# Folding a bias row and a corner product into one product, and moving half of the second norm's statistics

## The reference

```python
mod = (silu(c) @ wmod).reshape(8, 6, 1, -1)            # sa, ca, ga, sb, cb, gb
h = layernorm(x) * (1 + ca) + sa
attn = einsum('ds,td->st', w1, w2) * sparse_mask       # 1024 x 1024, non-zero near the diagonal
x = x + ga * gelu(einsum('bds,st->bdt', h, attn) + b2)
h = layernorm(x) * (1 + cb) + sb
P = h @ U1; H = P @ V1 + b1                            # 1024 -> 256 -> 2 x 2752
Z = (silu(gate) * up) @ U2; out = Z @ V2 + b2f         # 2752 -> 256 -> 1024
x = x + gb * out
```

## Time and profile before

| | |
|---|---|
| median of 3 runs | 1170.33 us (1170.17 to 1173.3) |
| profiled execution: its time / its span | 1172.08 / 1170.3 us |
| TensorE busy | 1142.7 us, 98% |
| weight loads / VectorE / ScalarE / GpSimd busy | 946.7 / 588.5 / 490.1 / 390.5 us |
| attention loop from batch 1 | about 97.5 to 251 us |
| low-rank loop | about 252.8 to 372 us |

### The profile page before, as it was taken

How to read it: one execution, slowest core, us unless ns; L and a number is a source line. 1 busy time by engine, 2 the same in 40 slices (tenths; PEclk the granted TensorE clock), 3 DMA queues, 4 the chain that set the end, 5 groups by cost and what they waited for, 6 DMA issues and landing times.

```text
span 1170.3 us, 15391 instructions
## 1 busy us (share of the span) xinstructions
PE 1142.7 (98%) x5883; PEld 946.7 (81%) x5883; DVE 588.5 (50%) x941; ACT 490.1 (42%) x789; POOL 390.5 (33%) x339
## 2 busy tenths in 40 slices
PE   5899999999999999999999999999999999999998
PEld 4668989987888788888888888888888888888886
DVE  3568777885663335444434444343443434344344
ACT  2137767777886544233224224223322432432331
POOL 1028998971113765302113031221302113021210
PEclk9899999999999999999999999999999999999999
DMA  9997888777536541501321040140123105013001
GB/s 359 394 348 261 305 328 323 252 259 251 220 140 219 164 164 73 180 1 72 97 84 73 20 160 1 73 155 26 72 66 115 56 16 180 1 73 109 35 1 72
DMA packets 57484, 169.59 MB, mean 145 GB/s; under 512 B 6208, under 2 KB 11072, under 8 KB 55360
## 3 DMA queue, kind: packets, MB, share of 16 engines
q1 hardware_dynamic: 57408, 168.57, 40.1%
HBM read 126.51 MB, written 42.04 MB: 144 GB/s over the span
## 4 chain that ended last, share of the span: by engine, by line
PE 88%; DMA 3%; SPq 2%; DVE 2%; POOL 2%; issue 1%; ACT 1%; DVEq 0%; POOLq 0%; ACTq 0%
PE bank L546 22%; PE bank L548 21%; PE bank L547 21%; PE bank L728 8%; PE bank L609 4%; PE bank L930 3%; PE bank L937 2%; PE bank L932 2%; PE bank L583 2%; DMA w2t_sb<-in_w2t 1%; PE bank L714 1%; POOL g L1603 1%; SPq L379 1%; POOL xs L1606 1%; PE bank L910 1%
## 5 line engine op out<-in xcount | busy, mean ns | idle before, releaser
L1169 ACT ACTIVATE act<-bank,b_sb 128x512 f32<-128x512 f32 (+1 forms) x176 | 121.3, 690 | 497.3 <-PE bank L548 481.4
L1518 DVE SCALAR_TENSOR_TENSOR act<-bank,b_sb,act 128x512 f32<-128x512 f32 (+1 forms) x176 | 132.0, 750 | 376.3 <-PE bank L548 353.2
L546 PE MATMUL bank<-pt,v_hi 128*128 128x512 f32 x688 | 268.6, 390 | 0.0
L547 PE MATMUL bank<-pt,v_hi 128*128 128x512 f32 x688 | 267.8, 389 | 0.0
L548 PE MATMUL bank<-pt,v_lo 128*128 128x512 f32 x688 | 267.6, 389 | 0.0
L1674 POOL TENSOR_TENSOR x2t<-gbb_bc,x2t 128x512 f32<-128x512 f32 x64 | 86.5, 1374 | 244.8 <-DMA x2t<-x_dram 244.8
L1528 DVE TENSOR_TENSOR act_lo<-act,act_hi 128x512 fp32r<-128x512 f32 (+1 forms) x176 | 160.4, 912 | 0.8
L546 PEld LDWEIGHTS bank<-pt,v_hi 128*128 128x128 f32 x688 | 129.1, 188 | 29.5 <-DVE act L1518 2.6
L548 PEld LDWEIGHTS bank<-pt,v_lo 128*128 128x128 f32 x688 | 129.2, 188 | 26.9
L547 PEld LDWEIGHTS bank<-pt,v_hi 128*128 128x128 f32 x688 | 129.2, 188 | 26.7
L546 PE MATMUL bank<-act_hi,u_hi 128*128 128x512 f32 x336 | 131.0, 390 | 0.7 <-DVE act_lo L1528 0.6
(11 more groups left out here) (134 smaller groups left out, 1663.3 us busy)
## 6 DMA issues: line engine op xcount, KB each, us to landing
xs<-in_x SPq DMA_DIRECT2D x32, 512.0 KB, 5.2
wm_sb<-in_wmod SPq DMA_DIRECT2D x8, 2048.0 KB, 10.8
x_dram<-xs SPq DMA_DIRECT2D x32, 512.0 KB, 5.3
xs<-x_dram SPq DMA_DIRECT2D x32, 512.0 KB, 5.9
x2t<-x_dram SPq DMA_DIRECT2D x32, 512.0 KB, 4.0
out<-x2t SPq DMA_DIRECT2D x31, 512.0 KB, 4.9
pt_dram<-pt_st SPq DMA_DIRECT2D x8, 1024.0 KB, 4.3
pt<-pt_dram SPq DMA_DIRECT2D x8, 1024.0 KB, 5.6
```

The lines of the kernel that those rows point to most:

```text
L546: nc.tensor.matmul(acc, s_hi, m_hi, start=start, stop=False)
L547: nc.tensor.matmul(acc, s_hi, m_lo, start=False, stop=False)
L1169: nc.scalar.activation(act[0:w, j % 2, :], bank[0:w, j % 2, :], ACT.Silu, bias=b1_sb[0:w, i, 0:1]).then_inc(silu_done, 1)
L1518: nc.vector.scalar_tensor_tensor(act[0:w, j % 2, :], up, b1_sb[0:w, i, 1:2], act[0:w, j % 2, :], ALU.add, ALU.mult).then_inc(act_done, 1)
```

## The change

It has two parts.

The first is in the attention loop, batches 1 to 7. The bias product used 16 of its 128 rows. Now the 70-column corner's first product (hi x hi) shares it. For the first half, rows 0 to 95 of `corner` hold a copy of `h_hi` of block 4 and rows 96 to 127 one-hot rows that pick the batch's bias; `fold` holds in the same rows `attn_hi`'s 70 columns and the bias of both parts. For the second half rows 32 to 127 and block 3 are used. ScalarE makes these copies (`corner_pick`, `corner_rows`, and `fold_rows` once), TensorE moves the bias rows into place once (`fold_turn`), GpSimd fills `fold`. The 32 rows left out of a corner are covered by the mask's check: two more scans (`CORNERS`). In batch 0 the old bias product stays; `beta` now lies in another place and is zeroed earlier.

The second part removes `stats2`: all four pieces of the second norm's tiles are measured from the tile loaded back, in the place of the loop where the other two were. SyncE's `next_x` no longer waits for `stats2`. After the attention loop SyncE issues `next_x2(NB + 3)` first, then the weight loads, and the stores of the gate tables one batch later.

```diff
+    KEPT, SPARE = 96, 32
+    CORNERS = [(FB // 2, HALF - REACH, HALF, slice(KEPT, P)), (FB // 2 - 1, HALF, HALF + REACH, slice(0, SPARE))]
...
             def next_x(t, n):
-                if n < 2:
-                    sp.wait_ge(bn2_done, (t - 3) * 4 + 2 * n + 2)
                 sp.wait_ge(x2_out[n], (t - 3) * 16 + 16)
...
+            def fold_turn(h):
+                pe.wait_ge(beta_lo_ready, h + 1)
+                pe.wait_ge(ga_first, h + 1)
+                rows = BETA_LO + NB
+                nc.tensor.matmul(bank[0:2 * NB, 6 + h, :], both[0:rows, :], beta[0:rows, h * HALF:(h + 1) * HALF],
+                                 start=True, stop=True).then_inc(fold_turned, 1)
...
+                toks = slice(n * P, (n + 1) * P)
...
+                if n == 0:
+                    pe.wait_ge(corner_ready[h], (2 + h) * b)
...
+                nc.tensor.matmul(bank[:, n, :], corner[:, h, toks], fold[:, h, :], start=False, stop=True,
                                  skip_group_check=True).then_inc(y_done, 1)
...
-                for i, (moving, weight) in enumerate(((h_hi, attn_hi), (h_hi, attn_lo), (h_lo, attn_hi))):
+                terms = [(h_hi, attn_hi), (h_hi, attn_lo), (h_lo, attn_hi)]
+                if b > 0 and part == CORNERS[h][:3]:
+                    del terms[0]
+                for i, (moving, weight) in enumerate(terms):
...
+            def corner_pick(b, h):
+                ae.wait_ge(y_done, (b - 1) * 8 + (h + 1) * TT)
...
+                rows = CORNERS[h][3]
+                nc.scalar.activation(corner[rows, h, :], pick[rows, b:b + 1].to_broadcast([SPARE, TOK]),
+                                     ACT.Copy).then_inc(corner_ready[h], 1)
+
+            def corner_rows(b, h):
+                i = b * FB + CORNERS[h][0]
+                ae.wait_ge(hi_ready, i + 1)
+                ae.wait_ge(y_done, (b - 1) * 8 + (h + 1) * TT)
+                for rows in ((slice(0, KEPT),), (slice(SPARE, 2 * SPARE), slice(2 * SPARE, P)))[h]:
+                    nc.scalar.activation(corner[rows, h, :], h_hi[rows, i % RING, :],
+                                         ACT.Copy).then_inc(corner_ready[h], 1)
...
             for b in range(1, NB):
                 hi(b, 4)
-                for k in range(5, FB):
-                    hi(b, k)
+                hi(b, 5)
+                corner_rows(b, 0)
+                hi(b, 6)
+                hi(b, 7)
...
                 lo(t, 5)
-                if b == 0:
-                    stats2(NB - 1, 0)
+                if b + 2 < NB:
+                    stats(t + 2, 0)
                 lo(t, 6)
+                if b + 2 < NB:
+                    stats(t + 2, 1)
```

More of the change, by code:

```diff
@@ L710, in y_end @@
                         y_part(b, u, part, False)
[L711 to L715, removed]
+                if b == 0:
+                    if n == 0:
+                        pe.wait_ge(pick_made, 7)
+                        pe.wait_ge(beta_lo_ready, h + 1)
+                    nc.tensor.matmul(bank[:, n, :], pick[:, b:b + 1].to_broadcast([P, P]),
+                                     beta[:, h * HALF:(h + 1) * HALF], start=False, stop=True,
+                                     skip_group_check=True).then_inc(y_done, 1)
+                    return
+                toks = slice(n * P, (n + 1) * P)
+                if whole:
+                    s, a, e, rest = CORNERS[h]
+                    nc.tensor.matmul(bank[:, n, a - h * HALF:e - h * HALF], h_hi[rest, (b * FB + s) % RING, toks],
+                                     attn_hi[rest, s, a:e], start=False, stop=False, skip_group_check=True)
+                if n == 0:
+                    pe.wait_ge(corner_ready[h], (2 + h) * b)
+                    if b == 1:
+                        pe.wait_ge(fold_made, 4)
+                        pe.wait_ge(fold_ready, h + 1)
+                nc.tensor.matmul(bank[:, n, :], corner[:, h, toks], fold[:, h, :], start=False, stop=True,
                                  skip_group_check=True).then_inc(y_done, 1)
@@ L979, in norm @@
                     ae.wait_ge(turned, (t - 1) * FB + c * 4 + 4)
-                if c == 0 and n not in pieces_of(t):
-                    ae.wait_ge(*source_in(t, n))
                 cols = slice(c * HALF, (c + 1) * HALF)
@@ L1097, in _ @@
             gelu(0, 6)
+            fold_rows(0)
             hi(1, 2)
             hi(1, 3)
+            fold_rows(1)
+            corner_pick(1, 0)
             gelu(0, 7)
@@ L1112, in _ @@
                 split(0)
+                corner_pick(b, 1)
                 gelu(b, 1)
+                corner_rows(b, 1)
                 norm(b + 1, 0, 1)
@@ L1120, in _ @@
                 split(2)
+                if b < NB - 1:
+                    corner_pick(b + 1, 0)
                 for k in range(4):
@@ L1274, in _ @@
                                              ALU.max, accum_out=off_any[:, n:n + 1]))
+            link(nc.vector.memset(off_any[:, len(off_band):], 0.0))
+            for n, (s, a, e, rest) in enumerate(CORNERS):
+                col = len(off_band) + n
+                link(nc.vector.tensor_scalar(off_junk[rest, 0:e - a], mask_sb[rest, s, a:e], 0.0, 0.0, ALU.not_equal,
+                                             ALU.max, accum_out=off_any[rest, col:col + 1]))
             nc.vector.tensor_reduce(off_max[:], off_any[:], AX.X, ALU.max).then_inc(off_known, 1)
@@ L1432, in _ @@
             add(0, 5)
-            stats2(0, 0)
             lo(1, 6)
@@ L1621, in _ @@
             pool.wait_ge(attn_mm, FB)
-            nc.gpsimd.memset(beta[:].bitcast(F32), 0.0).then_inc(beta_zeroed, 1)
+            nc.gpsimd.memset(fold[:].bitcast(F32), 0.0).then_inc(fold_made, 1)
+            pool.wait_ge(attn_hi_ready, FB)
+            for k, (h, rows) in enumerate(((0, slice(0, KEPT)), (1, slice(SPARE, 2 * SPARE)), (1, slice(2 * SPARE, P)))):
+                s, a, e, _ = CORNERS[h]
+                pool.wait_ge(fold_made, k + 1)
+                nc.gpsimd.tensor_copy(fold[rows, h, a - h * HALF:e - h * HALF],
+                                      attn_hi[rows, s, a:e]).then_inc(fold_made, 1)
+            pool.wait_ge(fold_made, 4)
             def weight_lo(m):
```

120 lines of the change are left out of this document (62 added, 58 removed).

## The result

The changed kernel takes 1177.70 us (median of 5 runs, 1176.94 to 1178.44), the kernel before 1170.33 in the same session: a ratio of 1.0053, 95% interval 1.0037 to 1.0069. It is slower by 7.4 us by the medians, 6.2 by the ratio, where 1163.9 was forecast. The profiled execution took 1178.44 with a span of 1176.6. One of the twelve executions of a later experiment, early_jump, took 3198.53 us and the other eleven 1171.21 to 1174.01; its ratio is that of the eleven.

A forecast was written before the change was run, and what follows sets the result against it. TensorE, busy 98% of the span, was taken to set the pace. Terms -6.2 - 3.7 + 2.5 + 1.0 = -6.4 us from the median 1170.33 gave 1163.9 (chance 0.50), range 1160.3 to 1167.8.

The forecast's parts named there:

- Removed products, -6.2: Attention batches 1 to 7: 56 fewer 70-column TensorE products at 0.11 us each, 6.2 us gained.
- The price of 0.11: Attention loop: each removed 70-column product saves a step of 0.11 us, not its listed duration of 0.19.
- Batch 7, +2.5 and clock +1.0: Last attention batch: ScalarE's copies delay norm and u1, 2.5 us (2.0 a TensorE wait); low clock after it, 1.0 more.
- Rival A: Last attention batch: ScalarE catches up, so TensorE has no wait there; -9.9, 1160.4 us; chance 0.17.
- ScalarE's copies hidden in batches 1 to 6, 0: Attention batches 1 to 6: ScalarE's added copies fall into its waits and cost 0; uncovered, up to 1.6 us a batch.
- The stall, -3.7: Low-rank loop, near 281: earlier loads of x2 remove TensorE's stall, 3.7 us gained, 1.95 of them idle, the rest clock.
- Rival C: Low-rank loop: a load still lands late once, or added VectorE pairs delay TensorE; 1166.5 to 1167.5 us; chance 0.15.
- D: Low-rank loop: loads become a loop of their own and batches wait for them; +18, 1182 us; chance 0.06.
- added statistics: Low-rank loop: two more VectorE pairs a batch (2.4 us) fit beside TensorE by 0.2 us; cost 0.

The follow-up runs named there:

- early_jump: Changed kernel with the code of the variant for a dense mask put behind the first batch; 1172.97 us, 1.0021 of before.
- after_moved_code: Changed kernel with 47 more TensorE products, never executed, in the jumped-over variant for a dense mask; 1171.17 us, 1.0003 of before.
- before_moved_code: Kernel before with 79 more TensorE products, never executed, in the jumped-over variant for a dense mask; 1175.5 us, 1.0041 of before.
- fold_alone: Kernel before with the change's first part alone, plus 48 unexecuted products that keep the place of the code behind the jump; 1169.90 us, 0.9993 of before.
- late_gates: after_moved_code with one group of VectorE's gate features moved from batch 5 to batch 6; 1168.10 us, 0.9975 of before.
- stats_alone: Kernel before with the change's second part alone; 1169.11 us, 0.9984 of before.
- loads_first: Kernel before with SP's order alone changed, loads of x2 ahead of weight loads and gate tables; 1168.31 us, 0.9978 of before.
- norm_ahead: after_moved_code with, in the last batch, ScalarE's norm ahead of the copies of h_hi rows and u1's first two splits behind them; 1172.01 us, 1.0008.
- loads_held: Changed kernel with SP's x2 loads, and two stores queued behind, held until TensorE's first low-rank product is done; one execution, 1175.1 us.

## Why the prediction was wrong

*The step that failed is the sum itself: it had no term for the jump behind the attention loop.* "What bounds the kernel now" read the steady batches, the last batch and the stall, and not the one wait for issue between the loops. The code ahead of the landing is 96 instructions shorter, all in all, which moved the jump's target from 162 to 66 modulo 256, and the end of a block came to lie eight products behind it. That cost 6.5 us in the changed kernel (after_moved_code) and as much code moved the other way cost 4.8 in the kernel before (before_moved_code): shown in both directions. It is no property of the change. In the traces, 4.22 are the wait; of the rest about 1.4 is low clock around it, a stretch of 6.8 us (0.8 of it inside the wait) against 3.4 us in after_moved_code, and 1.0 the low clock of batch 1, which is not shown to belong to it. Held against the two traces stretch by stretch, the forecast missed 6.7 us in the low-rank loop (+3.0 for -3.7), 2.9 in batch 7 and its jump (+5.5 for +2.6), 2.0 in batches 2 to 6 (-2.4 for -4.4) and 1.0 ahead of them.

*Removed products, -6.2.* The price of 0.11 held: in fold_alone steady batches take 20.97 to 20.99, 0.9 less than 21.90. But the steady rows of batches 3 to 5 were taken for all. In batch 5 VectorE's gate features lie in front of the last statistics pairs and of h_lo; before, TensorE had no wait there. With each batch up to 0.9 shorter it waited 0.80 for h_lo, and batch 6 took 22.55. late_gates brought it to 21.30. This is the second term that was missing: 1.3 us in batch 6 and 0.86 of wait at batch 7's start.

*Batch 7, +2.5 and clock +1.0.* The wait for the norm was right in place and size: 2.08 against 2.0, at 239.96. ScalarE's rows and TensorE's show it as computed, the three copies, the norms, the split and the last norm without a gap:

```profile
234.25 0.61 ACT L1086 ACTIVATE corner<-pick 32x512 fp32r<-32x512 f32 x1
235.37 1.29 ACT L1094 ACTIVATE corner<-h_hi 32x512 fp32r<-32x512 f32 x2
238.58 0.62 ACT L1100 ACTIVATE u_hi<-u_raw 128x512 fp32r<-128x512 f32 x1
239.10 0.80 ACT L1011 ACTIVATE nrm<-xs,shift,rstd 128x512 f32<-128x512 f32 x1
...
239.96 0.66 PE L613 MATMUL bank<-ident,nrm 128*128 128x128 f32 x4 [2.08 <-ACT nrm L1011]
```

Rival A is out. The other half of the term was wrong: u1 was to be whole at about 247.9, just ahead of the product and 0.5 us of the charge. It was whole at 246.58, 2.0 ahead of the product (248.54), since the last two pieces took 0.67 and 1.36 and not 3.46. The clock behind it is a term without a fixed size: 1.7 us here, 3.4 in late_gates behind 2.54, nothing in fold_alone behind 2.59. With the start's wait (0.86) and the longer jump (2.27 for 1.23) batch 7 lost 5.5.

*ScalarE's copies hidden in batches 1 to 6, 0.* Nearly right, but the cover is used up. Before, the norm for the transpose behind unit 3 ended 2.6 us ahead of it (172.48, 175.03); in batch 2 and batch 4 of the changed kernel that transpose comes 0.2 later than in batch 3 and only 0.05 behind the norm (173.38, 173.43 in batch 4; in batch 2 its weight load is listed with 0.38 of wait for nrm). That is most of the 0.6 us by which batches 2 to 5 are longer than in fold_alone.

*The stall, -3.7.* Right in size against the one trace of before (108.53 against 112.27 in stats_alone), and loads_first shows the cause that was argued, SP's order. By the medians it was worth 1.6 (stats_alone) and 2.6 (loads_first): the term took over all that one trace lost, low clock included, while most executions of before have no more low clock in all than those of these two kernels. What was not seen, too, is that it depends on when TensorE and the loads arrive: TensorE meets it neither in fold_alone nor in before_moved_code, with SP's old order. So the two parts of the change were not additive: the first part alone already had this gain.

*Rival C and D, added statistics.* Neither came: steps of 1.83 from 269.12 on, no wait for x_dram. (D's 2.6 to 10.3 us of landing were those of 16 loads and 4 stores; the loads alone took 3.2 to 9.6, median 6.5.)

*What a corrected sum gives.* With the code's place and both orders mended the change is worth 1170.87 - 1164.94 = 5.9 us, near the 6.4 of the forecast; that they meet is in part luck, since the terms came out otherwise than forecast. The two orders were not tried on the kernel before, whose trace shows none of the waits that they remove. after_moved_code, the change as it stands but for the place of the code, is level with before.

Why the jump alone costs 0.9 us in one trace (norm_ahead) and 2.5 in another (fold_alone) is shown in part: the packet of the landing block starts 1.25 us ahead of the last product in the one and 0.37 behind it in the other, and from its end on both take 1.7. Left open is what starts it earlier or later. SP's loads are not it (loads_held), nor the place of the code (late_gates 1.37, after_moved_code 2.37).

## What to carry to other kernels

Where an engine jumps over code that isn't run, ask how much work lies between the landing and the end of its block of 256 instructions (where the count starts is found by one shifted kernel). Here the next block came 5 to 6 us behind the landing: with less work than that left in the landing block, moving the code alone cost 4.8 us in one kernel and gave 6.5 in another, which has nothing to do with the edit that is timed. So put such code where the landing block is long, and keep loads out of that moment. To time an edit, hold the place of the code behind the jump fixed with instructions that aren't executed, and only then compare. When the pacing engine gets faster, look through all batches, not a steady one, for the place where a helper was already late, since that is where it is met first.

## What the runs showed of the hardware that was not expected

- Behind a taken jump TensorE had its first instructions after 0.9 to 2.5 us at the loop's end (4.09 near 97), and the next 256-instruction block 5.1 to 5.9 us after that; with SP's 512 KB loads held back, 3.1 us after it. The transfer of that block starts 2.8 to 4.6 us behind the landing beside the loads and 0.3 to 0.5 without them, and lasts 0.9 to 1.7 us.
- Half clock came in stretches of about 3.4 or 6.8 us (1.7 or 3.4 us lost). A wait of 2 us or more brought one in most traces (2.08, 2.37, 2.54, 3.71, 4.22) but not in all (2.59, 2.07 in early_jump, and 3.52 in before_moved_code). The wait of 1.5 to 1.6 near 97, which thirteen traces have, brought one in three of them (changed, stats_alone, before_moved_code). So the length of the wait alone doesn't tell.
